# Cross attention of a decoder layer: keeping each batch's scores in SBUF and taking their maximum there, instead of scoring twice

## The chip, the cores and the metric

The kernel runs on 1 core of one Trainium2 chip. The metric is the device time of one execution in microseconds (us), the median over runs. A profiled execution gives the trace from which all rows below come.

## What is computed

The whole decoder layer is self attention (an LSTM makes Gaussian weights), cross attention, and a mixture of four experts chosen per token. The change touches the cross attention alone:

```python
# x: (32, 56, 128), ctx_1024: (32, 1500, 128), 16 heads of 64
q = (Q @ WQ).reshape(N, ql, HEADS, DK)
k = (K @ WK).reshape(N, kl, HEADS, DK)
v = (V @ WV).reshape(N, kl, HEADS, DV)
compat = jnp.einsum('nqhk,nlhk->nhql', q, k) / math.sqrt(DK)
weights = jax.nn.softmax(compat, axis=3)
attn = jnp.einsum('nhqk,nkhv->nqhv', weights, v).reshape(N, ql, HEADS * DV)
return attn @ WO + bO
```

Q is the normalized x, K and V are both the context. The kernel folds WQ with WK and WV with WO, so per batch the queries are a 128 x 896 matrix (16 heads x 56 queries = 896 columns) which is multiplied with the context itself.

## The kernel before

There are 32 batches, worked in 16 pairs (112 tokens); batch b = 2i + k belongs to pair i. The context of a batch, 1500 rows, is cut into 12 chunks of 125 rows (CH = 12, CR = 125), and the 896 columns into two halves of 448. One call of `period(i, k)` on each engine is one batch; it runs over 12 slots, one for each chunk. The first and the last pair are written out, the others are a loop. Each engine has its own instruction stream, and all order between engines is by semaphores (`need(engine, name, value)` waits).

For one batch the kernel before does this:

- **The maximum, from a scoring pass of its own, one batch ahead.** TensorE (`side("max")`, L598) multiplies the queries of batch b+1 with the context in 21 pieces (7 blocks of 128 columns x 3 parts of 500 rows), with the queries on the partitions, so that VectorE (`read_max`, L1252) can reduce each piece along the free dimension. VectorE then makes a diagonal of the 896 maxima (`max_diag`, L1259), TensorE spreads it over all partitions (L603), and ScalarE stores it negated (`negate_max`, L969).
- **The scores.** ScalarE copies the negated maxima into the PSUM banks of a chunk (`seed`, L976), TensorE adds the scores on top (`scores`, L717: three products of the fp32r high and low parts for each half), and ScalarE takes the exponential from PSUM into one of four SBUF buffers (`probs`, L1033).
- **The weighing.** TensorE multiplies the exponentials with the context (`weigh`, L729), one chunk behind the scores. GpSimd adds the exponentials up for the denominators (L447, L452), 11 additions for each batch.
- **Work beside it**, placed by two strings of letters, one for each batch of a pair, `PLACES`: twelve words are the twelve slots, and four letters in a word are the places after TensorE's four half products of the slot. `m` is a max piece, `t` a piece of turning the next context (L590; ScalarE L898 makes its high part, VectorE L1139 its low part), `q` the next queries (L629), `s` the denominators (L609), `p` the projection (L617; VectorE L1290 adds the heads), `d` the spread. All of these share PSUM banks 6 and 7 in turn: a piece waits until the piece before it in its bank was read (`side_banks`).

ScalarE and VectorE also each take half of the weighed sum out of PSUM once for each batch (`take_u`, L996 and L1267), and split the next queries (`query_hi`, L963; `query_lo`, L1244).

## Time and profile before

| | |
|---|---|
| median of 3 runs | 1717.54 us (1717.15 to 1722.96) |
| the profiled execution: time, span of the core | 1721.62 us, 1719.5 us |
| TensorE busy over the span | 96% |
| ScalarE, VectorE, GpSimd busy | 53%, 49%, 46% |
| TensorE's granted clock, mean | 0.975 |

The cross attention takes the time from about 185 us to about 1612 us. A matmul's record covers its latency too, so two matmuls that follow each other overlap in the trace; what one costs TensorE is read from the start of one to the start of the next, or from the pieces of the chain.

### The profile page before, as it was taken

How to read it: one execution, taken by the hardware profiler on the slowest of the kernel's cores; microseconds unless marked ns; L12 is line 12 of the kernel's file. 1: busy time of each engine (PE TensorE's matmuls, PEld its weight loads, DVE VectorE, ACT ScalarE, POOL GpSimd, SP SyncE). 2: the span in 40 equal slices, each digit the busy share in tenths (PEclk: the TensorE clock that was granted, in tenths of full speed). 3: DMA queues.
4: the chain of work that ended last, by engine and by line, in shares of the span. 5: the costliest groups of instructions: out<-in, count | busy, mean ns of one | idle time of the engine just before them, and what ended most of it. 6: DMA issues, size and time to landing. Idle time of an engine off the chain costs nothing.

```text
span 1719.5 us, 25064 instructions
## 1 busy us (share of the span) xinstructions
PE 1647.4 (96%) x7783; PEld 1181.7 (69%) x7783; DVE 843.5 (49%) x1772; ACT 918.7 (53%) x1311; POOL 792.1 (46%) x414
## 2 busy tenths in 40 slices
PE   6876999999999999999999999999999999998997
PEld 3344677777777777777777777767677777776664
DVE  3349445454545444454545445454454545454345
ACT  3233565656565656555555556565656565655211
POOL 2003454545454555545455555454545454545410
PEclk9996899999999999999999999999999999999788
DMA  4000000000000000001010101000000000000000
GB/s 150 25 17 2 1 36 37 36 36 36 36 36 36 36 36 36 36 29 43 18 45 15 44 20 40 31 36 36 36 36 36 36 36 36 36 18 1 1 1 22
DMA packets 15052, 54.84 MB, mean 32 GB/s; under 512 B 919, under 2 KB 6122, under 8 KB 15022
## 3 DMA queue, kind: packets, MB, share of 16 engines
q1 hardware_dynamic: 15022, 54.46, 8.4%
q8 instruction: 17, 0.28, 0.1%
q14 instruction: 13, 0.11, 0.0%
HBM read 53.54 MB, written 0.92 MB: 32 GB/s over the span
## 4 chain that ended last, share of the span: by engine, by line
PE 87%; DVE 8%; ACT 2%; issue 1%; POOL 1%; DMA 0%; DVEq 0%; POOLq 0%; ACTq 0%
PE ps L729 32%; PE ps L717 26%; PE ps L598 9%; PE ps L617 3%; PE ps L629 3%; PE ps L779 3%; PE ps L609 3%; PE ps L590 2%; DVE max_diag L1259 2%; PE ps L524 1%; DVE max_parts L1252 1%; PE ps L603 1%; DVE xnorm L1099 1%; ACT arena L877 1%; ACT arena L880 1%
## 5 line engine op out<-in xcount | busy, mean ns | idle before, releaser
L452 POOL TENSOR_TENSOR arena<-arena,probs 125x896 f32<-125x896 f32 x320 | 677.6, 2118 | 546.8 <-ACT probs L1033 456.6
L729 PE MATMUL ps<-probs,ctx_nat 125*128 125x448 f32 x1536 | 685.7, 544 | 0.0
L1252 DVE TENSOR_REDUCE max_parts<-ps 128x1 f32<-128x500 f32 x672 | 451.6, 676 | 354.7 <-PE ps L598 347.2
L1033 ACT ACTIVATE probs<-ps 125x896 f32<-125x896 f32 x384 | 351.6, 916 | 474.3 <-PE ps L717 430.9
L598 PE MATMUL ps<-ctxT_hi,q_hi 128*128 128x500 f32 x672 | 365.1, 544 | 2.2 <-DVE max_parts L1252 1.3
L976 ACT ACTIVATE ps<-arena 125x896 f32<-125x896 f32 x384 | 354.1, 922 | 7.9
L729 PEld LDWEIGHTS ps<-probs,ctx_nat 125*128 125x128 f32 x1536 | 277.6, 191 | 95.8 <-issue 79.7
L717 PE MATMUL ps<-q_hi,ctxT_hi 128*125 128x448 f32 x768 | 331.2, 431 | 1.8 <-ACT ps L976 1.8
L717 PE MATMUL ps<-q_lo,ctxT_hi 128*125 128x448 f32 x768 | 282.8, 368 | 0.0
L717 PE MATMUL ps<-q_hi,ctxT_lo 128*125 128x448 f32 x768 | 281.7, 367 | 0.0
L717 PEld LDWEIGHTS ps<-q_hi,ctxT_hi 128*125 128x125 f32 x768 | 144.5, 188 | 70.0 <-issue 62.1
L598 PEld LDWEIGHTS ps<-ctxT_hi,q_hi 128*128 128x128 f32 x672 | 127.4, 190 | 82.2 <-DVE max_parts L1252 29.7
L717 PEld LDWEIGHTS ps<-q_lo,ctxT_hi 128*125 128x125 f32 x768 | 144.2, 188 | 42.5 <-issue 22.1
L717 PEld LDWEIGHTS ps<-q_hi,ctxT_lo 128*125 128x125 f32 x768 | 143.2, 186 | 14.2
L447 POOL TENSOR_TENSOR arena<-probs 125x896 f32<-125x896 f32 x32 | 68.4, 2139 | 149.0 <-ACT probs L1033 149.0
L1139 DVE TENSOR_TENSOR ctxT_lo<-ps,ctxT_hi 128x500 fp32r<-128x500 f32 x96 | 64.4, 670 | 131.0 <-ACT ctxT_hi L898 131.0
L1244 DVE TENSOR_TENSOR q_lo<-arena,q_hi 128x896 fp32r<-128x896 f32 x32 | 38.8, 1212 | 92.8 <-ACT q_hi L963 92.8
L898 ACT ACTIVATE ctxT_hi<-ps 128x500 fp32r<-128x500 f32 x96 | 56.3, 587 | 45.9 <-PE ps L590 45.9
L617 PEld LDWEIGHTS ps<-vo_w,arena 128*112 128x112 f32 x512 | 64.0, 176 | 23.8 <-issue 23.8
L1290 DVE SCALAR_TENSOR_TENSOR resid<-ps,sum_recip,resid 112x128 f32 (+1 forms) x128 | 44.3, 346 | 63.6 <-PE ps L617 63.6
L629 PEld LDWEIGHTS ps<-xT,qk_w 128*128 128x128 f32 x512 | 67.1, 196 | 11.0 <-issue 9.1
L629 PE MATMUL ps<-xT,qk_w 128*128 (+1 forms) x512 | 69.3, 281 | 0.6 <-ACT xT L859 0.6
(186 smaller groups left out, 1259.6 us busy)
## 6 DMA issues: line engine op xcount, KB each, us to landing
ctx_raw<-in_ctx_dram SPq DMA_DIRECT2D x32, 750.0 KB
ctx_nat<-in_ctx_dram SPq DMA_DIRECT2D x32, 750.0 KB
w_sb<-in_L_ffn_W_dram SPq DMA_DIRECT2D x1, 1024.0 KB
resid<-in_x_dram SPq DMA_DIRECT2D x1, 896.0 KB, 6.7
out_dram<-ctx_raw SPq DMA_DIRECT2D x4, 224.0 KB, 2.5
ctx_raw<-in_L_xattn_WQ_dram SPq DMA_DIRECT2D x1, 512.0 KB
w_sb<-in_L_xattn_WK_dram SPq DMA_DIRECT2D x1, 512.0 KB
w_sb<-in_L_xattn_WV_dram SPq DMA_DIRECT2D x1, 512.0 KB
```

The lines of the kernel that those rows point to most:

```text
L447: g.tensor_tensor(first_sum if k == 0 else summed, chunk[0], chunk[1], ALU.add).then_inc(s["prob_added"], 1)
L452: g.tensor_tensor(summed, first_sum if j == 2 and k == 0 else summed, chunk[j % NP], ALU.add).then_inc(s["prob_added"], 1)
L598: mm(ps[:, bank, 0:MC], q_hi[nk][:, block_ * 128:(block_ + 1) * 128], ctxT_hi[nk][:, part * MC:(part + 1) * MC], start=True, stop=True).th ...
L617: m = mm(ps[0:TOK, bank, n * D:(n + 1) * D], u_sum[:, h].rearrange("p b q -> p (b q)"), vo_w[:, h, :], start=True, stop=True)
L629: m = mm(ps[:, bank, n * TOK:(n + 1) * TOK], qk_w[:, 4 * which + n, :], xT[:, bass.ds(i + 1, 1), :].rearrange("p k t -> p (k t)"), start=T ...
L717: m = mm(score_ps[j % 2][:, half, :], cx[k][:, rows], q[k][:, cols], start=False, stop=True, skip_group_check=True)
L729: m = mm(usum_ps[:, half, :], ctx_nat[k][:, j, :], probs[j % NP][:, half, :], start=(j == 0), stop=(j == CH - 1))
L898: a(ctxT_hi[k][:, which * MC:(which + 1) * MC], ps[:, bank, 0:MC], ACT.Copy).then_inc(s["ctxT_hi_done"], 1)
L976: a(score_ps[j % 2], neg_max[k][0:CR], ACT.Copy).then_inc(s["seeded"], 1)
L1033: a(probs[j % NP][:], score_ps[j % 2], ACT.Exp, scale=SCALE).then_inc(s["prob_done"], 1)
L1139: v.tensor_tensor(ctxT_lo[k][:, part], ps[:, bank, 0:MC], ctxT_hi[k][:, part].bitcast(F32), ALU.subtract).then_inc(s["ctxT_lo_done"], 1)
L1252: v.tensor_reduce(max_parts[:, which:which + 1], ps[:, bank, 0:MC], AX.X, ALU.max).then_inc(s["max_read"], 1)
```

## The change

The scoring pass for the maximum goes away. Each batch's scores are made once, copied to a ring of 12 SBUF buffers, and everything after works in that ring:

- **TensorE.** The twelve `scores` of batch b+1 run during the weighing of batch b. At the start of a period `turn_max` transposes the running maxima (8 transposes) into banks 6 and 7, `spread_max` (8 small matmuls against an identity) writes the found maxima over all 125 partitions into the same two banks, where they stay until the last subtraction has read them. After a slot's `weigh` comes `scores` of the chunk after it.
- **ScalarE.** `keep_scores` copies the scores of a chunk from PSUM to the ring in place of `seed`; `exponential` works in place in the ring.
- **VectorE.** `run_maximum` takes the maximum of `run_max` and a ring buffer, 11 for each batch (the last one reads PSUM); `find_max` reduces the turned maxima; `subtract_max` subtracts the maxima, which lie in PSUM, from each ring buffer, 12 chunks.
- **Order within a period.** ScalarE does `exponential` of chunks 0 and 1, then for each slot j `keep_scores(b + 1, j)` and the exponentials in `EXPS_AT[j]`. VectorE does the first four subtractions, then for each slot j from 1 `run_maximum(b + 1, j)` and the subtractions in `SUBS_AT[j]`.
- **Work beside it.** `PLACES` has no `m` and no `d` any more; the first piece is in slot 6. Queries are made two pairs ahead. The first batch's scores stand before the first period, and the last period has no scores.

```diff
-        PLACES = ("m..m mssm ssmm mmpm .mpm mmpm mmpm mqmm mqqt ..dd qt.. t...",
-                  "m..m mm.m mm.m mm.m m.m. m.m. m.mt m.m. m.mt ..dd .... .t..")
+        PLACES = (".... .... .... .... .... .... .t.t .t.p .p.p .p.. .... ....",
+                  ".... .... .... .... .... .... .t.t .t.q .q.q .qss ss.. ....")
+        EARLY = 4
+        SUBS_AT = {1: (4, 5), 2: (6,), 3: (7, 8), 4: (9,), 5: (10, 11)}
+        EXPS_AT = {0: (2, 3), **SUBS_AT}
...
         def side_banks(i, k):
...
+            before = {SIDE + n: ("subbed", STEPS * (2 * i + k + 1)) for n in range(2)}
...
             def scores(b, k, j, half):
...
-                    need(pe, "seeded", CH * b + j + 1)
+                    need(pe, "copied", CH * b + j - 1)
+                    if j == 1:
+                        need(pe, "maxed", (CH - 1) * b)
...
+            def keep_scores(b, j):
+
+                need(act, "scored", CH * b + j + 1)
+                if j == CH - 1:
+                    need(act, "maxed", (CH - 1) * (b + 1))
+                need(act, "weighted", CH * (b - 1) + j + 1)
+                need(act, "prob_added", (CH - 1) * (b - 1) + max(j, 1))
+                a(ring[j], score_ps[j % 2], ACT.Copy).then_inc(s["copied"], 1)
+
+            def exponential(b, j):
+
+                for part in ((slice(0, 1), slice(1, 2)) if j == 0 else (slice(0, 2),)):
+                    need(act, "subbed", step_count(b, j, part.stop - 1))
+                    a(ring[j][:, part], ring[j][:, part], ACT.Exp, scale=SCALE).then_inc(s["prob_done"], 1)
...
+                exponential(b, 0)
+                exponential(b, 1)
                 for j in range(CH):
...
+                    if j:
+                        side_copies(i, k, j - 1)
+                    if not last:
+                        keep_scores(b + 1, j)
+                    for n in EXPS_AT.get(j, ()):
+                        exponential(b, n)
...
+                for half in range(2):
+                    turn_max(i, k, half)
+                if not last:
+                    for half in range(2):
+                        scores(b + 1, 1 - k, 0, half)
+                for half in range(2):
+                    spread_max(b, half)
+                if not last:
+                    for half in range(2):
+                        scores(b + 1, 1 - k, 1, half)
                 for j in range(CH):
...
                     for half in range(2):
...
+                        weigh(i, b, k, j, half)
                         beside(j, half)
                     for half in range(2):
...
+                        if 1 <= j < CH - 1 and not last:
+                            scores(b + 1, 1 - k, j + 1, half)
                         beside(j, 2 + half)
...
+            def run_maximum(b, j):
+
+                if j < CH - 1:
+                    need(dve, "copied", CH * b + j + 1)
+                else:
+                    need(dve, "scored", CH * b + j + 1)
...
+                v.tensor_tensor(run_max, ring[0] if j == 1 else run_max, ring[j] if j < CH - 1 else score_ps[j % 2], ALU.max).then_inc(s["maxed"], 1)
...
+                for half in range(2):
+                    find_max(b, half)
+                if not first:
+                    take_u(i, k)
+                for j in range(EARLY):
+                    subtract_max(b, j)
+                for j in range(1, CH):
+                    if not (last_pair and k == 1):
+                        run_maximum(b + 1, j)
+                    for n in SUBS_AT.get(j, ()):
+                        subtract_max(b, n)
+                    late_turns(i, k, j - 1)
...
+                    side_reads(i, k, j, range(4))
```

How the instructions stand shows it. In each row the brackets name the semaphores waited for; ring buffers carry the names `arena`, `wo_raw` or `ring` after the memory they lie in. ScalarE before, in batch 1 (written out): a seed, L976, and an exponential, L1033, in turn.

```order
L976 ACTIVATE ps<-arena 125x2x448 [waits s_neg_done,s_prob_done]
L1033 ACTIVATE probs<-ps 125x896 [waits s_prob_added,s_weighted,s_scored]
L969 ACTIVATE arena<-ps 128x448 [waits s_spread_ps] x2
L976 ACTIVATE ps<-arena 125x2x448 [waits s_neg_done,s_prob_done]
L1033 ACTIVATE probs<-ps 125x896 [waits s_prob_added,s_weighted,s_scored]
```

ScalarE after, batch 1 from its start to slot 5: L989 is `keep_scores` of batch 2 (chunks 0, 1, 2, ...), L995 is `exponential` of batch 1.

```order
L1014 ACTIVATE arena<-ps 128x8x56 [waits s_weighted]
L995 ACTIVATE arena<-arena 125x448 [waits s_subbed] x2
L995 ACTIVATE arena<-arena 125x896 [waits s_subbed]
L989 ACTIVATE arena<-ps 125x896 [waits s_prob_added,s_weighted,s_scored]
L995 ACTIVATE arena<-arena 125x896 [waits s_subbed] x2
L989 ACTIVATE arena<-ps 125x896 [waits s_prob_added,s_weighted,s_scored]
L995 ACTIVATE arena<-arena 125x896 [waits s_subbed]
L995 ACTIVATE wo_raw<-wo_raw 125x896 [waits s_subbed]
L989 ACTIVATE arena<-ps 125x896 [waits s_prob_added,s_weighted,s_scored]
L995 ACTIVATE ring<-ring 125x896 [waits s_subbed]
L989 ACTIVATE arena<-ps 125x896 [waits s_prob_added,s_weighted,s_scored]
L995 ACTIVATE ring<-ring 125x896 [waits s_subbed] x2
```

What moved: the copies of the next batch now stand between the exponentials of this one, and each exponential waits for VectorE. VectorE before, in batch 1:

```order
L1267 COPY arena<-ps 128x8x56 [waits s_weighted]
L1252 TENSOR_REDUCE max_parts<-ps 128x1 [waits s_max_ps] x16
L1139 TENSOR_TENSOR ctxT_lo<-ps,ctxT_hi 128x500 [waits s_ctxT_hi_done]
L1252 TENSOR_REDUCE max_parts<-ps 128x1 [waits s_max_ps] x3
L1256 TENSOR_REDUCE max_all<-max_parts 128x7 [waits s_diag_done,s_max_read]
L1259 TENSOR_TENSOR max_diag<-ident,max_all 128x896 [waits s_spread_ps,s_max_found]
```

VectorE after, batch 1 from the third full subtraction: L1268 is `run_maximum` of batch 2 (chunks 1 to 5), L1282 is `subtract_max` of batch 1.

```order
L1282 TENSOR_TENSOR arena<-arena,ps 125x896 [waits s_spread_ps,s_copied] x3
L1268 TENSOR_TENSOR arena<-arena 125x896 [waits s_run_turned,s_copied]
L1282 TENSOR_TENSOR arena<-arena,ps 125x896 [waits s_spread_ps,s_copied]
L1282 TENSOR_TENSOR wo_raw<-wo_raw,ps 125x896 [waits s_spread_ps,s_copied]
L1268 TENSOR_TENSOR arena<-arena 125x896 [waits s_maxed,s_copied]
L1282 TENSOR_TENSOR ring<-ring,ps 125x896 [waits s_spread_ps,s_copied]
L1268 TENSOR_TENSOR arena<-arena 125x896 [waits s_maxed,s_copied]
L1282 TENSOR_TENSOR ring<-ring,ps 125x896 [waits s_spread_ps,s_copied] x2
L1268 TENSOR_TENSOR arena<-arena 125x896 [waits s_maxed,s_copied]
L1282 TENSOR_TENSOR ring<-ring,ps 125x896 [waits s_spread_ps,s_copied]
```

What moved: the 21 reductions from PSUM are gone; a maximum that waits for ScalarE's copy stands ahead of the subtractions for which ScalarE's exponentials wait. TensorE before, in slot 8 of batch 1: a turning piece (L590) waits for the reading of a max piece.

```order
L729 MATMUL ps<-probs,ctx_nat 128x448
L590 MATMUL ps<-ident,ctx_raw 128x125 [waits s_max_read]
L590 MATMUL ps<-ident,ctx_raw 128x125 x3
L717 MATMUL ps<-q_hi,ctxT_hi 125x448 [waits s_seeded]
L717 MATMUL ps<-q_lo,ctxT_hi 125x448
```

TensorE after, slots 6 and 7 of batch 1: L738 is `weigh`, L588 the turning piece, L704 `scores` of batch 2.

```order
L738 MATMUL ps<-ring,ctx_nat 128x448
L588 MATMUL ps<-ident,ctx_raw 128x125 [waits s_ctx_in1,s_subbed]
L588 MATMUL ps<-ident,ctx_raw 128x125 x3
L704 MATMUL ps<-q_hi,ctxT_hi 125x448 [waits s_copied]
...
L738 MATMUL ps<-ring,ctx_nat 128x448
L588 MATMUL ps<-ident,ctx_raw 128x125 [waits s_ctxT_lo_done]
L588 MATMUL ps<-ident,ctx_raw 128x125 x3
```

What moved: the first turning piece now waits for the last subtraction of the batch, with the scores of chunk 7 behind it, and the third waits for VectorE to have read the first.

## Rows read from the trace of the kernel before

**Rows 1.** The page: span, then busy time of each engine.
```profile
span 1719.5 us, 25064 instructions
PE 1647.4 (96%) x7783; PEld 1181.7 (69%) x7783; DVE 843.5 (49%) x1772; ACT 918.7 (53%) x1311; POOL 792.1 (46%) x414
```

**Rows 2.** Busy times in one pair of batches: stretch, length, engines, granted clock.
```profile
708.55:798.16 89.61, 89.35 (x409) 65.69 (x408) 44.14 (x77) 52.95 (x67) 46.57 (x23) 1.00 0.09 34
```

**Rows 3.** Chain that ended last, same pair: shares by line; pieces (start, us).
```profile
by line: PE ps L729 39.1%; PE ps L717 31.5%; PE ps L598 10.9%; PE ps L629 4.1%; PE ps L617 3.9%; PE ps L609 3.1%; PE ps L590 2.5%; DVE max_diag L1259 2.5%; PE ps L603 1.2%; DVE max_parts L1252 0.8%; issue 0.3%; DVE max_all L1256 0.2%; DVEq 
...
727.22 1.23 PE ps L717 x6
741.34 1.01 PE ps L629 x8
...
755.16 1.51 PE ps L729 x4
```

**Rows 4.** The same view of 715 to 722 us.
```profile
717.92 0.23 PE ps L598
718.15 0.61 PE ps L717 x3
718.75 0.69 PE ps L609 x8
```

**Rows 5.** Groups by line, 400 to 1600 us: busy us, mean ns; idle.
```profile
L452 POOL TENSOR_TENSOR arena<-arena,probs 125x896 f32<-125x896 f32 x268 | 567.1, 2116 | 458.5 <-ACT probs L1033 380.3 <-PE ps L609 76.8
L1252 DVE TENSOR_REDUCE max_parts<-ps 128x1 f32<-128x500 f32 x546 | 367.1, 676 | 290.3 <-PE ps L598 289.3
L976 ACT ACTIVATE ps<-arena 125x896 f32<-125x896 f32 x322 | 297.0, 922 | 6.5
L1033 ACT ACTIVATE probs<-ps 125x896 f32<-125x896 f32 x323 | 295.7, 916 | 399.7 <-PE ps L717 359.6 <-POOL arena L452 35.0 <-POOL arena L447 5.1
L1139 DVE TENSOR_TENSOR ctxT_lo<-ps,ctxT_hi 128x500 fp32r<-128x500 f32 x76 | 51.0, 671 | 104.7 <-ACT ctxT_hi L898 104.7
L963 ACT ACTIVATE q_hi<-arena 128x896 fp32r<-128x896 f32 x25 | 23.7, 949 | 0.0
L1267 DVE COPY arena<-ps 128x448 f32<-128x448 f32 x27 | 16.6, 614 | 9.4 <-PE ps L729 9.4
```

**Rows 6.** Timeline around 657 us: start us, us, engine, instruction.
```profile
656.60 1.09 DVE L1259 TENSOR_TENSOR max_diag<-ident,max_all 128x896 fp32r<-128x896 f32 x1
657.35 2.29 POOL L452 TENSOR_TENSOR arena<-arena,probs 125x896 f32<-125x896 f32 x1 [2.35 <-ACT probs L1033]
```

**Rows 7.** Timeline around 880 us.
```profile
878.95 2.10 POOL L452 TENSOR_TENSOR arena<-arena,probs 125x896 f32<-125x896 f32 x1 [1.33 <-ACT probs L1033]
879.80 2.21 DVE L1259 TENSOR_TENSOR max_diag<-ident,max_all 128x896 fp32r<-128x896 f32 x1
```

**Rows 8.** Timeline around 887 us, for the step from one engine to another.
```profile
885.03 0.90 ACT L1033 ACTIVATE probs<-ps 125x896 f32<-125x896 f32 x1
886.08 2.10 POOL L452 TENSOR_TENSOR arena<-arena,probs 125x896 f32<-125x896 f32 x1 [1.63 <-ACT probs L1033]
886.82 0.94 ACT L963 ACTIVATE q_hi<-arena 128x896 fp32r<-128x896 f32 x1
...
887.78 1.35 DVE L1244 TENSOR_TENSOR q_lo<-arena,q_hi 128x896 fp32r<-128x896 f32 x1 [5.18 <-ACT q_hi L963]
```

**Rows 9.** Busy times around a stall late in the cross attention; columns as in 2.
```profile
1560.00:1568.00 8.00, 8.00 (x30) 5.24 (x28) 3.25 (x11) 5.74 (x7) 4.93 (x4) 1.00 0.00 0
1568.00:1576.00 8.00, 3.75 (x10) 2.18 (x9) 6.46 (x17) 2.27 (x3) 3.77 (x3) 0.69 0.01 3
1576.00:1584.00 8.00, 8.00 (x31) 5.76 (x29) 1.57 (x1) 4.01 (x5) 4.62 (x3) 0.88 0.00 0
```

More of the change, by code:

```diff
@@ L581, in spread_mask, with turn, sums @@
                 mm(ps[:, mask_bank(e), 0:GT], pick_e[:, e, :], onehotT[n], start=True, stop=True).then_inc(s["mask_ps"], 1)
+            def turn(i, k, which, bank):
+                if which == 0:
+                    need(pe, f"ctx_in{k}", 16 * (i + 2))
+                for c in range(TG):
+                    m = tr(ps[:, bank, c * CR:(c + 1) * CR], ctx_in[k][:, which * TG + c, :], ident[0:CR, 0:CR])
+                m.then_inc(s["ctxT_ps"], 1)
+            def sums(pair, which, bank):
+                if which == 0:
+                    need(pe, "prob_added", (CH - 1) * 2 * (pair + 1))
+                for n in range(4):
+                    m = mm(ps[0:TOK, bank, n:n + 1], prob_sum[:, 4 * which + n].rearrange("p b q -> p (b q)"), ones[0:CR, 0:1], start=True, stop=True)
+                m.then_inc(s["sums_ps"], 1)
@@ new lines, in project, with query @@
+            def project(pair, which, bank):
+                if which == 0:
+                    need(pe, "u_act", 2 * (pair + 1))
+                    need(pe, "u_dve", 2 * (pair + 1))
+                for n in range(4):
+                    h = 4 * which + n
+                    m = mm(ps[0:TOK, bank, n * D:(n + 1) * D], u_sum[:, h].rearrange("p b q -> p (b q)"), vo_w[:, h, :], start=True, stop=True)
+                m.then_inc(s["projected"], 1)
+            def query(pair, which, bank):
+                for n in range(4):
+                    m = mm(ps[:, bank, n * TOK:(n + 1) * TOK], qk_w[:, 4 * which + n, :],
+                           xT[:, bass.ds(pair, 1), :].rearrange("p k t -> p (k t)"), start=True, stop=True)
+                m.then_inc(s["q_ps"], 1)
@@ L619, in side @@
+                    turn(i, k, which, bank)
+                elif what == "sums":
+                    sums(i, which, bank)
+                elif what == "project":
+                    project(i - 1, which, bank)
+                elif what == "query":
+                    query(i + 2, which, bank)
                 elif what == "tokens":
@@ L626, in side @@
                     spread_mask(0, which)
-                elif what == "query":
-                    for n in range(4):
-                        m = mm(ps[:, bank, n * TOK:(n + 1) * TOK], qk_w[:, 4 * which + n, :],
-                               xT[:, bass.ds(i + 1, 1), :].rearrange("p k t -> p (k t)"), start=True, stop=True)
-                    m.then_inc(s["q_ps"], 1)
             def beside_first(u):
@@ new lines, in find_max, with subtract_max @@
+            def find_max(b, half):
+                need(dve, "run_turned", 2 * b + half + 1)
+                need(dve, "spread_ps", 2 * (b - 1) + half + 1)
+                v.tensor_reduce(max_all[:, 4 * half:4 * half + 4], ps[0:QB, SIDE + half, 0:4 * CR].rearrange("p (n l) -> p n l", n=4),
+                                AX.X, ALU.max).then_inc(s["max_found"], 1)
+            def subtract_max(b, j):
+                need(dve, "copied", CH * b + j + 1)
+                for part in ((slice(0, 1), slice(1, 2)) if j == 0 else (slice(0, 2),)):
+                    need(dve, "spread_ps", 2 * b + part.stop)
+                    v.tensor_tensor(ring[j][:, part], ring[j][:, part], ps[0:CR, SIDE + part.start:SIDE + part.stop, 0:HALF],
+                                    ALU.subtract).then_inc(s["subbed"], 1)
@@ L1375, in side_reads @@
                 for what, which, bank in slot_work(i, k, j, places):
-                    if what == "max":
-                        read_max(i, k, which, bank)
-                    elif what == "sums":
-                        invert_sums(i - 1, which, bank)
+                    if what == "sums":
+                        invert_sums(i, which, bank)
                     elif what == "project":
```

340 lines of the change are left out of this document (128 added, 212 removed).

## The prediction

> **What bounds the kernel now.** I read the page first: TensorE is busy for 96% of the span and the others for about half [rows 1]. A busy TensorE can hide waits, so next comes one pair of batches by itself: 89.6 us, 44.8 for a batch, at the full granted clock, with ScalarE busy 53, GpSimd 47 and VectorE 44 us of it [rows 2]. The chain of that stretch says what the time is spent on: all but some 4% is matmul after matmul [rows 3]. The shares are costs without latency: six score products (one chunk) 1.23 us, four weighing passes (one chunk) 1.51 [rows 3], one max piece 0.23, four denominators 0.69 [rows 4]. For one batch: scores 12 x 1.23 = 14.8; weighing 12 x 1.51 = 18.1; max pieces 21 x 0.23 = 4.8; half of each pair's turning (2.5% of 89.6), denominators, projection and queries, 6.1; spread and the wait for `max_diag`, about 1. That is 44.8. TensorE is the bound, and nothing else comes near.
>
> **The change by sums.** TensorE loses the max pieces and the spread (-4.8, -0.5) and gains 8 transposes and 8 small matmuls. A turning transpose costs 0.09 (2.5% of 89.6 us over 24) [rows 3]; the small ones are not in the trace, between nothing and the same, together 0.8 to 1.6, and I take 1.3. TensorE's own work becomes 40.8 us. ScalarE trades each seed (0.92) for a copy of the same size. GpSimd keeps 11 additions of 2.12 [rows 5]. VectorE loses 21 x 0.68 and gains 11 maxima and 12 subtractions of 896 elements. From SBUF such an operation is 1.09 [rows 6]; from PSUM, 500 elements take 0.671 and 448 take 0.614 [rows 5], which carried on to 896 is also 1.1. With its other work VectorE has about 33 us. If sums decided, TensorE would still be the bound and the kernel 4 us faster for each batch. They do not, because of the order.
>
> **The change by its order.** Let time 0 be the end of batch b-1's last weighing. No engine can pass it: the maximum of b needs all its scores, and every exponential of b needs the maximum. I follow the three written orders from there. A copy or an exponential is 0.92, a maximum or a subtraction 1.09.
>
> *Turn-over, 12.6 us.* Chunk 10's copy goes into a buffer that the weighing frees just before, so copy 10, maximum 10 and maximum 11 (3.1) run against TensorE's scores 11 and weighing 11 (2.7): with the steps, a wait of 0.8. Then: first four transposes with their latency 0.65; two `find_max` reductions, as L1252, 1.36; `take_u` 0.61; subtraction 0 in halves 1.22; subtraction 1 1.09; exponential 1 0.92. The copy of the next chunk 0 overwrites buffer 0, which GpSimd's first addition still reads: 2.12 and 0.15 for the step to GpSimd (885.93 to 886.08) [rows 8]. Then copy 0, exponentials 2 and 3, copy 1: 3.67. Sum 12.4, and 0.2 for steps of 0.02 to 0.15 between engines [rows 8]. The scores of chunks 0 and 1 (2.5) hide in it.
>
> *Ping-pong, 24.0 us.* From slot 1 to 5 ScalarE and VectorE work in turn and hardly ever together: copy j frees maximum j, ahead of the subtractions; these free the exponentials, and they stand ahead of copy j+1. Slots 1, 3 and 5 cost maximum, two subtractions, exponential, copy: 5.11. Slots 2 and 4, with one subtraction, 4.02. That is 23.4, and 0.6 for ten steps. TensorE needs only 2.74 for a slot, but its scores j+1 wait for copy j-1, so it goes at 4.7. Subtraction 11 ends at 34.7. Only now may the first turning piece use bank 6, with scores 7 behind it: weighing 7 begins at 36.9.
>
> *Tail.* TensorE is the bound again: 5 weighings 7.55, 4 scores 4.9, one turning piece 0.4; projections of the first batch of a pair 3.5, or queries 4.0 and denominators 2.8 of the second. Twice a piece needs the bank of a turning piece that VectorE reads only behind its next maximum: after weighing 7, copy 7, maximum 7 and the low part (0.92 + 1.09 + 0.67 and steps) make 3.1, and the same once more in slot 8. The tail is 22.6 or 25.9.
>
> Batches end at 59.5 and 62.8, mean **61.1 us** where it was 44.8.
>
> *A lock.* `run_maximum` reads two SBUF operands while GpSimd adds. The nearest thing is `max_diag`: 1.09 alone, where a GpSimd addition that starts behind it takes 2.29 for 2.10 [rows 6], but 2.21 when the addition has begun, ending 1.0 after that ends [rows 7]. So a maximum can wait for the rest of an addition: nothing to 2.1 each. Where two exponentials precede it, the addition that the first one frees is just ending (0.1 to 0.3); after a single one it has about 1.2 left. Slots 1 to 5: 0.3, 0.1, 1.2, 0.1, 1.2, so 2.9; bounds 0 and 10.5. The Trainium skill, "SBUF — State Buffer", section "SBUF: two separate sides", says that VectorE with two SBUF inputs and GpSimd hold a shared port pair alternately, each for a whole instruction. By that rule the batch is 64.0, without it 61.1; both rows agree with it.
>
> *The clock.* Where TensorE is busy for 3.75 of 8 us, the granted clock falls to 0.69, and is 0.88 in the next 8 us: about 6.8 us at 1.2 instead of 2.4 GHz [rows 9]. Here TensorE sits idle for some 4.7 us in slot 6 and 3 us twice later. One such fall in a batch costs at most 3.4 us, none costs nothing, two 6.8; as part of the low time falls on waits, I take 1.5.
>
> **Sum.** 61.1 + 2.9 + 1.5 = 65.5 a batch, +20.7 for 31 of them, +642. The last period has no scores: 12 x 1.51 and its turn-over, about 23 us, where the old one has 12 x 2.74 = 33: -10. At the start, 12 scored chunks take the place of 21 exposed reductions of 0.68: 14.8 against 14.2, +1. The profiled execution took 1721.6 (span 1719.5), 4 over the median: 1721.6 + 633 - 4 = **2350 us**.
>
> **Rivals.**
> - *The sums decide* (the other side). If the twelve buffers let ScalarE copy so far ahead that the ping-pong hides, a batch is 40.8 and the kernel 1717.5 - 31 x 4 + a few, about 1600. For it: every engine's sum is under 41. Against: copy j+1 stands behind the exponentials of slot j. It decides only if slots 1 to 5 take under 2.8 us each; the smallest has 4.0 us of work in sequence. 4%.
> - *The ping-pong alone.* The bank waits (6.2) and the lock (2.9) turn out hidden, and the clock stays full: 54.9 a batch, +10.1 x 31 - 9, about 2020; halfway cases up to 2200. Against: the waits are in the orders of the program. 7%.
> - *The clock stays low.* At 1.2 GHz TensorE's 40.8 us become 82 and it is the bound: +37 x 31, up to 2870. For it: with 41 us of work in 61, TensorE waits far more than anywhere in the loop before, and one long stall cost the clock [rows 9]. Against: at 1.2 GHz it would be busy all the time, and in such a stretch the clock came back to full within 8 us [rows 9]. A mixture above 2480: 9%. The Trainium skill, "TensorE: Matmul & The Clock Gate", section "What's actually happening", says that the throttled clock is the default and activity releases it; the fall and the return in rows 9 agree.
> - *Nothing changes* (the two effects cancel): 1%.
>
> **Chances and range.** The forecast has 79%: slower, 2200 to 2480. Its low end leaves out lock and clock (-91 and -46) and a little more for a wait that is shorter; its high end has a second fall of the clock in each batch or 4 us more of lock waits. That is also the range for 8 in 10. A difference under 0.5% (9 us) can't be told from none here. Faster 4%, same 1%, slower 95%.
>
> **What would show it.** In the new profile: a pair takes 120 to 135 us; VectorE's idle time before `run_maximum` ends mostly with ScalarE's copy, and ScalarE's before the exponentials with VectorE's subtraction, 2 us each, five times a batch; `run_maximum` has a mean above 1.09 us and subtractions of 1.1; TensorE waits over 4 us for the subtraction ahead of the turning piece of slot 6; a granted clock below 1. I am wrong if ScalarE's copies run ahead of VectorE (a pair near 82 us), if maxima from SBUF take their 1.09 throughout, or if the clock's mean is under 0.8.

## The result and the profile after

| | before | after |
|---|---|---|
| median of 4 runs each | 1717.43 us | 2399.09 us (2394.02 to 2409.38) |
| ratio after : before, 95% interval | | 1.3966 (1.3912 to 1.402) |
| the profiled execution: time, span | 1721.62, 1719.5 us | 2409.38, 2407.7 us |

Slower by 40%; forecast were 2350 us and a range of 2200 to 2480. First the page of the changed kernel: span, busy times, the granted clock of TensorE in 40 slices, the chain's shares by engine, then three groups (count, busy us, mean ns, idle us before them and what ended it).

```profile
span 2407.7 us, 24704 instructions
PE 1805.5 (75%) x7555; PEld 1245.1 (52%) x7555; DVE 1299.6 (54%) x1868; ACT 893.1 (37%) x1279; POOL 869.8 (36%) x414
PEclk9978888898889898888989888998889888889778
issue 36%; PE 29%; DVE 17%; ACT 12%; POOL 3%; DVEq 1%; ACTq 1%; DMA 0%; POOLq 0%
L1268 DVE TENSOR_TENSOR arena<-arena,ring 125x896 f32<-125x896 f32 x160 | 184.2, 1151 | 415.5 <-ACT ring L989 415.4
L1268 DVE TENSOR_TENSOR arena<-arena 125x896 f32<-125x896 f32 x128 | 198.3, 1549 | 328.5 <-ACT arena L989 328.2
L995 ACT ACTIVATE ring<-ring 125x896 f32<-125x896 f32 x192 | 182.4, 950 | 363.1 <-DVE ring L1282 359.9
```

TensorE fell from 96% to 75% of a longer span [rows 1], and no other engine is above 54%: nothing is full, so engines wait for each other. The groups name the pair. `run_maximum` (L1268) waits 415 and 328 us for ScalarE's copies (L989), and the exponentials (L995) wait 363 us for VectorE's subtractions (L1282). One pair of batches, with the columns of [rows 2]:

```profile
1257.90:1391.00 133.10, 99.11 (x396) 68.47 (x394) 72.68 (x84) 51.33 (x65) 51.86 (x22) 0.88 0.06 23
```

133.1 us for 89.6 [rows 2], at a granted clock of 0.88 instead of 1.00. ScalarE's busy time is about what it was, VectorE's rose from 44 to 73 us. Two slots of one batch, from the timeline (start us, us, engine, instruction, idle time before it and what ended it):

```profile
1409.50 0.95 ACT L995 ACTIVATE ring<-ring 125x896 f32<-125x896 f32 x1 [2.42 <-DVE ring L1282]
1410.36 0.90 ACT L989 ACTIVATE arena<-ps 125x896 f32<-125x896 f32 x1
1410.61 2.10 POOL L453 TENSOR_TENSOR arena<-arena,ring 125x896 f32<-125x896 f32 x1 [0.19 <-ACT ring L995]
...
1411.38 2.28 DVE L1268 TENSOR_TENSOR arena<-arena 125x896 f32<-125x896 f32 x1 [1.91 <-ACT arena L989]
...
1413.59 2.07 DVE L1282 TENSOR_TENSOR ring<-ring,ps 125x896 f32<-125x896 f32 x2
1414.69 1.95 ACT L995 ACTIVATE ring<-ring 125x896 f32<-125x896 f32 x2 [3.44 <-DVE ring L1282]
1415.80 4.99 POOL L453 TENSOR_TENSOR arena<-arena,ring 125x896 f32<-125x896 f32 x2 [3.08 <-ACT ring L995]
1416.55 0.90 ACT L989 ACTIVATE arena<-ps 125x896 f32<-125x896 f32 x1
1417.50 0.74 PE L704 MATMUL ps<-q_hi,ctxT_hi 128*125 128x448 f32 x1 [3.20 <-ACT arena L989]
1417.57 1.27 DVE L1268 TENSOR_TENSOR arena<-arena 125x896 f32<-125x896 f32 x1 [1.91 <-ACT arena L989]
```

This is the ping-pong: VectorE sits idle 1.91 us until the copy ends (1411.26), takes the maximum and two subtractions, while ScalarE sits idle 3.44; ScalarE does two exponentials and the next copy, while VectorE sits idle 1.91. The maximum that starts at 1411.38 takes 2.28 us and ends 0.95 after the GpSimd addition that had begun before it (1410.61 + 2.10 = 1412.71), as `max_diag` did in [rows 7]. The later part of the same batch:

```profile
1426.13 0.64 PE L588 MATMUL ps<-ident,ctx_raw 125*128 125x125 f32 x4 [3.04 <-DVE ring L1282]
...
1429.11 2.97 DVE L1255 TENSOR_TENSOR q_lo<-arena,q_hi 128x896 fp32r<-128x896 f32 x1
...
1431.64 0.92 ACT L989 ACTIVATE ring<-ps 125x896 f32<-125x896 f32 x1 [1.20 <-PE ps L738]
1432.67 1.09 DVE L1268 TENSOR_TENSOR arena<-arena,ring 125x896 f32<-125x896 f32 x1 [0.59 <-ACT ring L989]
1433.68 1.25 DVE L1150 TENSOR_TENSOR ctxT_lo<-ps,ctxT_hi 128x500 fp32r<-128x500 f32 x2
1434.41 1.10 PE L588 MATMUL ps<-ident,ctx_raw 125*128 125x125 f32 x4 [2.89 <-DVE ctxT_lo L1150]
```

A turning piece waits 2.89 us for the low part (L1150), which stands behind the maximum, which waits for the copy, which waits for the weighing. TensorE's granted clock around it, by stretches of 8 us with the columns of [rows 2]:

```profile
1418.00:1426.00 8.00, 5.09 (x10) 2.66 (x8) 6.08 (x5) 2.71 (x3) 4.87 (x2) 0.67 0.00 0
1426.00:1434.00 8.00, 5.39 (x18) 3.83 (x18) 5.51 (x4) 4.58 (x6) 4.92 (x2) 0.76 0.00 0
1434.00:1442.00 8.00, 7.05 (x22) 5.40 (x22) 2.06 (x6) 1.01 (x2) 0.00 (x0) 0.60 0.00 0
1442.00:1450.00 8.00, 5.65 (x26) 4.92 (x27) 3.79 (x10) 0.49 (x1) 0.00 (x0) 0.79 0.00 0
```

The clock is low in every one of these stretches, also where TensorE is the bound (7.05 of 8 us busy at 0.60). The forecast's one fall of the clock in some batches is here a mixture of 1.2 and 2.4 GHz over the second half of the batch. Last, what TensorE waited for in the loop, 400 to 1600 us (us in total, times, longest); 18 batches end in it:

```profile
PE ps L704 <- ACT arena L989: 127.3, 62, 3.2
PE ps L588 <- DVE ring L1282: 70.8, 18, 5.6
PE ps L588 <- DVE ctxT_lo L1150: 52.5, 18, 2.9
PE ps L609 <- DVE ctxT_lo L1150: 26.5, 9, 2.9
PE ps L604 <- DVE ctxT_lo L1150: 26.0, 9, 2.9
```

By batch: 7.1 us for copies, 3.9 for the last subtraction, and two bank waits (a turning, query or projection piece that waits until VectorE has read the piece before it in its bank) of 2.9.

### The profile page after: what moved, and what is told of

Read it like the earlier page. It is cut to its first block, busy times and chain, and to the rows that moved or that the text cites. A ratio compares the mean times of both kernels' runs of the same rounds, so it can differ in the third digit from the quotient of the medians.

```text
span 2407.7 us, 24704 instructions
## 1 busy us (share of the span) xinstructions
PE 1805.5 (75%) x7555; PEld 1245.1 (52%) x7555; DVE 1299.6 (54%) x1868; ACT 893.1 (37%) x1279; POOL 869.8 (36%) x414
## 4 chain that ended last, share of the span: by engine, by line
issue 36%; PE 29%; DVE 17%; ACT 12%; POOL 3%; DVEq 1%; ACTq 1%; DMA 0%; POOLq 0%
PE ps L704 8%; DVE ring L1282 8%; PE ps L738 7%; ACT arena L989 5%; POOL arena L453 3%; PE ps L609 3%; ACT arena L995 3%; DVE arena L1282 2%; PE ps L588 2%; PE ps L797 2%; PE ps L595 2%; DVE wo_raw L1282 1%; ACT ring L989 1%; ACT wo_raw L989 1%; DVE arena L1268 1%
## 5 line engine op out<-in xcount | busy, mean ns | idle before, releaser
L453 POOL TENSOR_TENSOR arena<-arena 125x896 f32<-125x896 f32 x128 | 289.9, 2265 | 1085.2 <-ACT arena L995 1081.2
L704 PE MATMUL ps<-q_hi,ctxT_hi 128*125 128x448 f32 x768 | 376.2, 490 | 226.3 <-ACT arena L989 221.3
L453 POOL TENSOR_TENSOR arena<-arena,ring 125x896 f32<-125x896 f32 x192 | 445.5, 2320 | 204.6 <-ACT ring L995 197.0
L1268 DVE TENSOR_TENSOR arena<-arena,ring 125x896 f32<-125x896 f32 x160 | 184.2, 1151 | 415.5 <-ACT ring L989 415.4
L738 PE MATMUL ps<-ring,ctx_nat 125*128 125x448 f32 x768 | 376.8, 616 | 0.0
L1268 DVE TENSOR_TENSOR arena<-arena 125x896 f32<-125x896 f32 x128 | 198.3, 1549 | 328.5 <-ACT arena L989 328.2
L989 ACT ACTIVATE ring<-ps 125x896 f32<-125x896 f32 x192 | 175.7, 915 | 456.1 <-PE ps L738 408.7
L704 PEld LDWEIGHTS ps<-q_hi,ctxT_hi 128*125 128x125 f32 x768 | 167.8, 218 | 331.6 <-ACT arena L989 312.8
L704 PE MATMUL ps<-q_hi,ctxT_lo 128*125 128x448 f32 x768 | 325.4, 424 | 0.0
L704 PE MATMUL ps<-q_lo,ctxT_hi 128*125 128x448 f32 x768 | 325.2, 423 | 0.0
L995 ACT ACTIVATE ring<-ring 125x896 f32<-125x896 f32 x192 | 182.4, 950 | 363.1 <-DVE ring L1282 359.9
L738 PE MATMUL ps<-arena,ctx_nat 125*128 125x448 f32 x640 | 285.1, 571 | 3.4 <-ACT arena L995 1.1
L588 PE MATMUL ps<-ident,ctx_raw 125*128 125x125 f32 x384 | 92.1, 387 | 202.1 <-DVE ring L1282 114.8
L738 PEld LDWEIGHTS ps<-ring,ctx_nat 125*128 125x128 f32 x768 | 164.7, 229 | 92.0 <-issue 87.9
L995 ACT ACTIVATE arena<-arena 125x896 f32<-125x896 f32 (+1 forms) x192 | 153.5, 824 | 158.1 <-DVE arena L1282 158.0
L1282 DVE TENSOR_TENSOR ring<-ring,ps 125x896 f32<-125x896 f32 x192 | 201.1, 1074 | 0.0
L588 PEld LDWEIGHTS ps<-ident,ctx_raw 125*128 125x128 f32 x384 | 65.6, 201 | 259.9 <-DVE ctxT_lo L1150 109.2
L704 PEld LDWEIGHTS ps<-q_hi,ctxT_lo 128*125 128x125 f32 x768 | 172.1, 224 | 19.5
L704 PEld LDWEIGHTS ps<-q_lo,ctxT_hi 128*125 128x125 f32 x768 | 171.2, 223 | 20.0 <-issue 8.7
L738 PEld LDWEIGHTS ps<-arena,ctx_nat 125*128 125x128 f32 x640 | 126.3, 203 | 100.1 <-issue 63.9
L989 ACT ACTIVATE arena<-ps 125x896 f32<-125x896 f32 x160 | 144.8, 905 | 76.0 <-POOL arena L453 69.5
L1282 DVE TENSOR_TENSOR arena<-arena,ps 125x896 f32<-125x896 f32 (+1 forms) x192 | 167.0, 924 | 9.5 <-PE ps L726 9.3
```

The costliest lines, as they stand in the source:

```text
L453: g.tensor_tensor(summed, chunk[0] if j == 1 else summed, chunk[j], ALU.add).then_inc(s["prob_added"], 1)
L588: m = tr(ps[:, bank, c * CR:(c + 1) * CR], ctx_in[k][:, which * TG + c, :], ident[0:CR, 0:CR])
L704: m = mm(score_ps[j % 2][:, half, :], cx[k][:, rows], q[k][:, cols], start=(n == 0), stop=(n == 2))
L738: m = mm(usum_ps[:, half, :], ctx_nat[k][:, j, :], ring[j][:, half, :], start=(j == 0), stop=(j == CH - 1))
L989: a(ring[j], score_ps[j % 2], ACT.Copy).then_inc(s["copied"], 1)
L995: a(ring[j][:, part], ring[j][:, part], ACT.Exp, scale=SCALE).then_inc(s["prob_done"], 1)
```

## The experiments

Ten kernels, each a change of the changed kernel (2399 us). Beside them on their chips the kernel before took 1721.5 us (first four), 1722.09 (next four, median of 13) and 1722.05 (last two). All are single runs, except the last two of the middle four; the four runs of the changed kernel span 15 us, so a difference of that size between single runs shows nothing. Where a batch's parts are named, they are those of the table behind the last experiment.

**The maximum behind the subtractions (order only).**

```diff
                 for j in range(1, CH):
-                    if not (last_pair and k == 1):
-                        run_maximum(b + 1, j)
                     for n in SUBS_AT.get(j, ()):
                         subtract_max(b, n)
+                    if not (last_pair and k == 1):
+                        run_maximum(b + 1, j)
                     late_turns(i, k, j - 1)
```

> Only the order on VectorE changes: in each slot of a period the subtractions stand ahead of run_maximum; instructions, sizes and counts are the same. Order theory: the exponentials of a slot then need not wait for the copy and the maximum, so slots 1 to 5 (26 us in the new profile) fall to about 15 to 17 us, a batch from 66.5 to 56 to 58 us, the kernel to 2060 to 2160 us. Rival, VectorE's amount of work or its lock with GpSimd is what costs: the same instructions take the same time, 2370 to 2430 us.

Measured: **2097.61 us**, 301 less. Nothing but the order of two calls changed. Its groups of maxima:

```profile
L1268 DVE TENSOR_TENSOR arena<-arena,ring 125x896 f32<-125x896 f32 x160 | 259.6, 1622 | 350.5 <-ACT ring L989 350.4
L1268 DVE TENSOR_TENSOR arena<-arena 125x896 f32<-125x896 f32 x128 | 202.2, 1579 | 87.5 <-ACT arena L989 85.5
```

The wait of the second group (chunks 1 to 4, in the slots of the ping-pong) fell from 328 to 88 us; the first group's (chunks 6 to 10) lies mostly in the tail and went from 415 to 351. The ping-pong went from 26.05 to 14.2 us a batch, and the tail took 2.4 of that back. The lock went on: the first group's mean rose from 1.15 to 1.62 us.

**Maxima from PSUM, at the same place.** They still wait for the copy, and TensorE's next scores now wait for them.

```diff
                     need(pe, "copied", CH * b + j - 1)
-                    if j == 1:
-                        need(pe, "maxed", (CH - 1) * b)
+                    if j == 0:
+                        need(pe, "maxed", (CH - 1) * b - 1)
+                    elif j != 2:
+                        need(pe, "maxed", (CH - 1) * b + max(j - 2, 0))
...
-                v.tensor_tensor(run_max, ring[0] if j == 1 else run_max, ring[j] if j < CH - 1 else score_ps[j % 2], ALU.max).then_inc(s["maxed"], 1)
+                v.tensor_tensor(run_max, ring[0] if j == 1 else run_max, score_ps[j % 2], ALU.max).then_inc(s["maxed"], 1)
```

> run_maximum waits for the copy as before but reads the chunk's scores from PSUM instead of the ring, so it has one SBUF operand; TensorE writes a score bank again only when it was also read by the maximum. Order theory: run_maximum has 1.1 us throughout, 3 us less in slots 1 to 5 and about 1 later, a batch 62 to 64 us, the kernel 2260 to 2330 us. Rival, the lock is the main cost: most of the 22 us that a batch lost come back, under 2000 us.

Measured: **2226.16 us**, 173 less and a little below the range, at a clock of 0.940 where the changed kernel had 0.871. The maxima took 1.09 us. The ping-pong got 3.05 us a batch shorter, 95 us in all, which is the lock; the rest of the gain lies mostly in the tail, at a higher clock (0.96 and 0.91 for 0.90 and 0.84) and with waits for low parts as long as before (6.1 us a batch for 5.8). Why the clock was higher here is not shown.

**Small additions.** Ten of a batch's eleven GpSimd additions add only 8 columns, so most of the denominators is left out; the first addition, for which ScalarE's copy waits, is whole.

```diff
-                    g.tensor_tensor(summed, chunk[0] if j == 1 else summed, chunk[j], ALU.add).then_inc(s["prob_added"], 1)
+                    (g.tensor_tensor(summed, chunk[0], chunk[j], ALU.add) if j == 1 else g.tensor_tensor(summed[:, 0:1, 0:8], summed[:, 0:1, 0:8], chunk[j][:, 0:1, 0:8], ALU.add)).then_inc(s["prob_added"], 1)
```

> Leaves out work: of GpSimd's 11 additions for each batch the first is whole, the other ten add 8 columns only, so the denominators are not the reference's. Every wait stays. Order theory: the lock's part goes, in the maxima and in query_lo (2.97 us in the new profile where it is 1.09 alone), together 4 to 6 us a batch: 2210 to 2290 us. Rival, the lock or GpSimd is the main cost: under 2000 us. Rival, neither matters because VectorE catches up: 2370 to 2430 us.

Measured: **2308.25 us**, 91 less: missed. The lock was gone (the two groups on its page):

```profile
L1268 DVE TENSOR_TENSOR arena<-arena,ring 125x896 f32<-125x896 f32 x160 | 174.8, 1093 | 509.7 <-ACT ring L989 509.5
L1268 DVE TENSOR_TENSOR arena<-arena 125x896 f32<-125x896 f32 x128 | 139.8, 1092 | 328.5 <-ACT arena L989 328.2
```

but its granted clock was 0.860, lower than the changed kernel's. By itself this run could not say whether the lock is worth only 91 us or the clock took some of it back; the ninth and tenth kernels were made for that.

**The low parts first.** `late_turns` ahead of the maximum and the subtractions of its slot.

```diff
                 for j in range(1, CH):
+                    late_turns(i, k, j - 1)
                     if not (last_pair and k == 1):
...
                         subtract_max(b, n)
-                    late_turns(i, k, j - 1)
```

> Only the order on VectorE changes: in each slot the low parts of the turned context stand ahead of run_maximum and the subtractions. Order theory of the tail: the third turning piece waits 1 us less and the second query or projection piece not at all (2.9 in the new profile), 3.5 to 4.5 us a batch, 2260 to 2300 us. Rival, the tail is TensorE's work at the low clock, and the waits only hide in it: 2370 to 2410 us.

Measured: **2181.32 us**, 218 less, more than expected. TensorE's waits for low parts, of the same stretch as above (20 batches here):

```profile
PE ps L588 <- DVE ctxT_lo L1150: 17.0, 17, 1.6
PE ps L604 <- DVE ctxT_lo L1150: 5.0, 10, 0.5
```

That is 1.1 us a batch for 5.8, so 4.7 x 31 = 146 us are the waits. The other 70 are not waits of this kind. The ping-pong is what it was (26.05), and the tail got 7.1 us a batch shorter while its clock rose (0.94 for 0.90 and 0.84), so a bank wait seems to cost its own length and, behind it, some matmuls at 1.2 GHz. That the wait is what lowers the clock is argued, not shown.

**TensorE kept busy in its waits.** 81 small matmuls a batch into an unused part of a bank. The expectations say 97, which is wrong: the numbers of `WARMERS` add up to 81, each of which is two passes in the trace (12577 instructions of TensorE for 7555, 162 more in each of 31 batches).

```diff
+        WARMERS = (0, 7, 0, 10, 6, 15, 15, 14, 14, 0, 0, 0)
...
                         weigh(i, b, k, j, half)
+                        if half == 1 and not last:
+                            for n in range(WARMERS[j]):
+                                mm(ps[:, 4, HALF:512], ident[:], ident[:, 0:512 - HALF], start=False, stop=False, skip_group_check=True)
                         beside(j, half)
```

> Adds work: where TensorE waited 1.2 to 3.2 us in slots 1 and 3 to 8 it makes 6 to 15 small matmuls (64 columns, into unused columns of PSUM bank 4), 97 in a batch. Nothing else changes. Clock as a cost of its own: the granted clock rises from 0.87 towards 1 and the tail of a batch (29.7 us where its work and waits at the full clock make 24.3) gets 4 to 6 us shorter: 2210 to 2290 us. Rival, the low clock only fills waits: 2390 to 2430 us, since the small matmuls take some time.

Measured: **2337.0 us**, 62 less, between the two theories, at a clock of 0.947. More work made the kernel faster, so the clock does cost time, and it costs it in the tail: the ping-pong stayed at 26.1 us. How much it costs in all, this run leaves open, since the small matmuls take time too.

**Subtractions, low parts, maximum: both orders together.**

```diff
                 for j in range(1, CH):
-                    if not (last_pair and k == 1):
-                        run_maximum(b + 1, j)
                     for n in SUBS_AT.get(j, ()):
                         subtract_max(b, n)
                     late_turns(i, k, j - 1)
+                    if not (last_pair and k == 1):
+                        run_maximum(b + 1, j)
```

> The two changes of order on VectorE together: in each slot subtractions, then low parts, then run_maximum; the same instructions. Apart they took 301 and 218 us off 2399. Order theory: both waits go, and with them much of the time at the low clock, 1850 to 1980 us; the lock remains. Rival, they overlap: not under 2040 us.

Measured: **1875.71 us**, 523 less, about the sum of the two orders (301 + 218). Of the 680 us that the change cost, three quarters go by moving one call behind two others.

**The maximum before the copy.** The written orders are those of the changed kernel. The maximum reads PSUM as soon as a chunk is scored, and the copy waits for it (run e7_max_before_copy). TensorE's waits are those of the second experiment.

```diff
                 need(act, "scored", CH * b + j + 1)
-                if j == CH - 1:
-                    need(act, "maxed", (CH - 1) * (b + 1))
+                if j:
+                    need(act, "maxed", (CH - 1) * b + j)
...
-                if j < CH - 1:
-                    need(dve, "copied", CH * b + j + 1)
-                else:
-                    need(dve, "scored", CH * b + j + 1)
+                need(dve, "scored", CH * b + j + 1)
                 if j == 1:
+                    need(dve, "copied", CH * b + 1)
...
-                v.tensor_tensor(run_max, ring[0] if j == 1 else run_max, ring[j] if j < CH - 1 else score_ps[j % 2], ALU.max).then_inc(s["maxed"], 1)
+                v.tensor_tensor(run_max, ring[0] if j == 1 else run_max, score_ps[j % 2], ALU.max).then_inc(s["maxed"], 1)
```

> The order on VectorE and ScalarE is that of the changed kernel. Only what run_maximum reads changes: the chunk's scores in PSUM as soon as they are made, with the copy to the ring behind it (for every chunk, as the changed kernel does it for the last). So VectorE no longer waits for ScalarE's copy, and the lock goes. Order theory: slots 1 to 5 are no ping-pong any more, TensorE (40.8 us of work for a batch) is the bound but for the turn-over: 44 to 47 us a batch, 1700 to 1800 us. Rival, the copy that now waits for the maximum is a ping-pong of its own: over 2000 us.

Measured: **1731.63 us** (median of 10 runs), ratio to before 1.0054 (1.0032 to 1.0075). One of the ten took 2916.48 us and is left out of the comparison, the others 1728.57 to 1735.80; its clock was 0.895, no trace of it exists, and its cause is open. VectorE in the slots of the ping-pong, from its timeline:

```profile
1236.35 1.08 DVE L1282 TENSOR_TENSOR arena<-arena,ps 125x896 f32<-125x896 f32 x1
1237.35 1.08 DVE L1282 TENSOR_TENSOR wo_raw<-wo_raw,ps 125x896 f32<-125x896 f32 x1
1238.35 1.08 DVE L1268 TENSOR_TENSOR arena<-arena,ps 125x896 f32<-125x896 f32 x1
1239.34 1.08 DVE L1282 TENSOR_TENSOR ring<-ring,ps 125x896 f32<-125x896 f32 x1
1240.34 1.08 DVE L1268 TENSOR_TENSOR arena<-arena,ps 125x896 f32<-125x896 f32 x1
```

No idle time at all: a maximum every 2.0 to 3.0 us, where it was 4.2 to 6.2. The order of VectorE's program is the same as in the slow kernel. Two things differ, the lock is gone and the maximum no longer waits for ScalarE's copy; the second experiment has the first of them alone, at 2226 us, so the wait for the copy is worth the other 494, with what the clock gave back in them.

**Both: the maximum before the copy, and behind the subtractions and low parts.** The edits of the last two together.

> As e7_max_before_copy, and in each slot on VectorE subtractions, low parts, then run_maximum. If the waits that are left in slots 6 to 8 go, a batch comes to 42.5 to 45 us and the kernel to 1650 to 1720 us, faster than the kernel before. If the turn-over (about 11 us, with 5 us of TensorE's work in it) stays the bound, 1720 to 1780 us.

Measured: **1687.39 us** (4 runs, 1683.72 to 1691.38), ratio to before **0.9801 (0.9758 to 0.9843)**: it beats both kernels, the kernel before by some 2%. Its page, and one pair (columns of [rows 2]):

```profile
span 1681.9 us, 25214 instructions
PE 1541.8 (92%) x7555; PEld 1084.7 (64%) x7555; DVE 1142.8 (68%) x1868; ACT 867.3 (52%) x1279; POOL 810.9 (48%) x414
```
```profile
1235.80:1323.60 87.80, 83.64 (x394) 59.96 (x393) 62.43 (x83) 49.64 (x65) 47.87 (x22) 1.00 0.09 35
```

The idea of the change, scores made once, is sound: 87.8 us a pair for 89.6. TensorE is busy for 83.6 of them, where the prediction's sum for a pair was 81.6.

**The two missed ones together: small additions and the small matmuls,** with the edits shown and the same part left out as in the third experiment.

> The changed kernel with both edits of the two kernels that fell between their theories: 10 of the 11 GpSimd additions of a batch add 8 columns only (so the output misses most of the denominators), and 97 small dummy matmuls a batch are added in TensorE's waits. Alone the first gave 2308 us at a granted clock of 0.860, the second 2337 us at 0.947. Theory (the lock's saving of the first was partly eaten by a lower clock): with the clock held up the two savings together are larger than their sum of 153 us: 2150 to 2220 us, clock above 0.93. Rival (the small additions save 91 us and no more, whatever the clock): 2240 to 2260 us.

Measured: **2165.95 us**, 233 less, where the two alone gave 91 and 62. Its page's busy times and clock:

```profile
PE 2085.8 (96%) x12577; PEld 1653.1 (76%) x12577; DVE 1131.4 (52%) x1868; ACT 890.0 (41%) x1279; POOL 179.0 (8%) x414
PEclk9979999999999999999999999999999999999989
```

Beside the small matmuls the small additions are worth 2337 - 2166 = 171 us. 95 of them are the lock in the ping-pong, 3.05 us a batch, the same as without the small matmuls. The rest is in the tail. Alone, the small additions made the tail of a pair's second batch longer, with the same number of matmuls and at a lower clock (one such tail of the changed kernel, then one of the third; columns of [rows 2]):

```profile
1357.87:1390.95 33.08, 27.13 (x128) 20.86 (x127) 11.74 (x14) 8.91 (x13) 3.27 (x2) 0.84 0.00 0
1437.88:1473.34 35.46, 29.57 (x128) 23.01 (x127) 9.67 (x15) 8.85 (x13) 0.00 (x0) 0.74 0.00 0
```

In the mean of both batches the tail got 0.7 us longer, which took back some 20 of the 95 us. Not all of the 171 is the lock, though: from the fifth kernel to this one the tail's clock rose too (0.93 and 0.98 to 1.00). And the small matmuls (L778) make 25% of the chain that ended last here, so they can cost time themselves; what this kernel shows of the clock's cost is a lower bound:

```profile
PE ps L778 25%; PE ps L739 23%; PE ps L705 20%; PE ps L610 3%; PE ps L605 3%; DVE arena L1286 2%; PE ps L801 2%; PE ps L596 2%; PE ps L589 2%; DVE arena L1272 2%; PE ps L719 2%; ACT arena L999 1%; PE ps L525 1%; ACT ring L993 1%; PE ps L727 1%
```

**Maxima from PSUM with the small matmuls.**

> The changed kernel with maxima that wait for the copy as before but read the scores from PSUM, and the 97 small dummy matmuls a batch. Alone the first gave 2226 us at a granted clock of 0.940. Theory (what the reading from PSUM gave beyond the small additions was the clock, so with the clock held up both come to about the same time): 2160 to 2230 us, within 40 us of the kernel with small additions and dummy matmuls; the dummy matmuls give it little, since its clock is high already. Rival (the dummy matmuls give the same 62 us whatever else is changed): 2164 us here while the kernel with small additions stays at 2246.

Measured: **2214.3 us**, 12 less than without them, which two single runs can't tell from nothing and which fits the theory (the clock was high already, 0.940), but 48 us from the ninth, a little outside the 40 expected. Turn-over and ping-pong are the same in both; each tail is 1.0 us longer here, 31 of the 48 us. What differs in it includes the `q_lo` operation (two SBUF inputs in both), which has a mean of 2.47 us here and 1.08 there, and TensorE's wait for the maxima, 0.7 us a batch; how the 1.0 us divides was not tried.

**The parts of a batch in the kernels whose maximum waits for the copy.** Means over the whole batches from 400 to 1600 us, in us, with the tail's granted clock in brackets. A batch is divided at the start of the first reduction of `find_max`, the end of copy 1 and the end of copy 6. The first part, most of the turn-over, is 10.8 in all of them.

| | ping-pong | tail, first batch of a pair | tail, second batch |
|---|---|---|---|
| the changed kernel | 26.05 | 27.7 (0.90) | 32.8 (0.84) |
| 1: maximum behind the subtractions | 14.2 | 31.7 (0.84) | 33.6 (0.87) |
| 2: maxima from PSUM | 23.0 | 26.3 (0.96) | 30.1 (0.91) |
| 3: small additions | 23.0 | 26.5 (0.92) | 35.5 (0.74) |
| 4: low parts first | 26.05 | 22.2 (0.94) | 24.1 (0.94) |
| 5: small matmuls | 26.1 | 27.3 (0.93) | 28.7 (0.98) |
| 6: both orders | 14.2 | 24.3 (0.93) | 25.8 (0.96) |
| 9: small additions, small matmuls | 23.0 | 24.8 (1.00) | 27.6 (1.00) |
| 10: maxima from PSUM, small matmuls | 23.0 | 25.8 (1.00) | 28.6 (1.00) |

The ping-pong goes by the order and the lock alone: it is the same at a clock of 0.84 as at 0.95 (changed and fifth kernel), and at 0.86 as at 1.00 (third and ninth). What the clock costs lies in the tail, and the changed kernel's own trace shows it: its first batches have two kinds of tail, with the same matmuls and the same waits for low parts, 4.1 us apart (columns of [rows 2]):

```profile
1427.79:1458.18 30.39, 23.82 (x94) 17.78 (x93) 16.11 (x28) 6.78 (x9) 3.27 (x2) 0.79 0.01 1
1294.73:1320.99 26.26, 19.70 (x94) 14.19 (x93) 16.10 (x28) 6.79 (x9) 3.26 (x2) 0.96 0.01 1
```

## Why the prediction held, point by point

**The sums do not decide, the order does: right.** The first rival named the ping-pong as what stood against it. With the lock gone and the clock held up (ninth experiment, its 81 added matmuls included) the kernel took 2166 us; the forecast's order terms alone, 61.1 a batch, give 1722 + 16.3 x 31 - 9 = 2218. The batches of that kernel were 58.6 and 61.5 us for 59.5 and 62.8.

**The parts of one batch.** The batch whose rows stand above runs from the end of one last weighing (1390.10) to the next (1456.71), 66.6 us; it is the first of a pair, forecast at 59.5 + 2.9 + 1.5 = 63.9.

| | forecast | measured |
|---|---|---|
| turn-over, to the end of copy 1 | 12.6 | 11.6 |
| ping-pong with lock, to the end of copy 6 | 24.0 + 2.9 | 26.1 |
| tail | 22.9 + 1.5 of clock | 28.9 |

This batch has one of the longer tails: four of the nine first batches in the loop are like it, five are 4.1 us shorter, and the second batches have the longest. Over the loop, divided as in the table above, a mean batch has 10.8 + 26.05 + 30.3. The forecast, divided so (the 0.8 and 0.65 ahead of `find_max` go to the tail before), has 11.15 + 26.9 + 27.5. So the first two parts came out 1.2 us under and the tail 2.8 over, 1.6 a batch or some 50 us in all: the number is closer than its terms, because the errors lay on both sides.

- *Turn-over and ping-pong.* Both a little shorter than forecast. Instructions that follow each other on VectorE or ScalarE start about 0.1 us before the recorded end of the one ahead (exponential 1409.50 + 0.95 = 1410.45, copy at 1410.36), which the sum counted in full, and the step of 0.12 (1411.26 to 1411.38) lies within the 0.02 to 0.15 assumed.
- *The lock.* The five maxima of the slots took 1.45, 1.25, 2.28, 1.27 and 2.26 us, so 0.36, 0.16, 1.19, 0.18 and 1.17 above 1.09: 3.1 for the forecast's 0.3, 0.1, 1.2, 0.1, 1.2. As a mean of the loop the ping-pong is 3.05 us longer than without the lock. That the addition is what they wait for is shown by the third experiment (1.09 throughout), that the reading from SBUF matters by the second. The Trainium skill, "SBUF — State Buffer", section "SBUF: two separate sides", says that VectorE with two SBUF inputs and GpSimd hold the pair alternately, each for a whole instruction; both experiments agree.
- *The bank waits.* Forecast 3.1 each, measured 2.9, two in each batch.
- *The clock: right in sign, mis-sized.* The term was 1.5 us a batch (one fall in some batches). The nearest thing to a measurement is the step from the third to the ninth experiment: 142 us, at least 4.6 a batch, within the bounds of 0 to 6.8. The mean tail is 4.3 above a forecast without clock, about the same. The term that was mis-sized is the number of falls: the estimate took one stall as one fall, in some batches; the rows show the low clock in all stretches from 1418 to 1450, where waits of 2 to 3 us come again and again. That these keep it low is argued, though filling them raised it to 0.988. The Trainium skill, "TensorE: Matmul & The Clock Gate", section "What's actually happening", says that the throttled clock is the default and activity releases it. A kernel made faster by added matmuls (62 us here, 142 with the small additions) agrees with it.
- *Lock and clock do not add.* The forecast has 2.9 + 1.5 = 4.4 a batch, 136 us; together they measured 233. Removed one at a time they gave 91 and 62; the prediction's ledger, like the expectations of the third and fifth experiments, treated them as independent terms. The lock's part in the ping-pong does add, 3.05 us with or without the small matmuls; the tail is where the two meet.

So 2399 came out 49 above the forecast: lock and clock 97 over, the order 52 under, and 4 because the forecast is against a median of 1717.5, and these steps against the 1722 of the kernel before beside them. These are single runs, and the 233 includes `q_lo`, which the forecast's lock leaves out.

**The signs.** A pair took 133 us (forecast 120 to 135). Idle before maxima and exponentials 1.9 to 3.4 us. The turning piece of slot 6 was to wait over 4 us: 3.04 in the batch shown, 3.9 as a mean, 5.6 at most, so this sign was just missed; the low clock lengthened the matmuls ahead of it and so ate some of the wait. The maxima's means were 1.15 and 1.55 us, above 1.09, the subtractions' 1.07, and the clock's 0.871 lies below 1 and above 0.8, as said. Not foreseen was `q_lo`, whose 2.97 us show the lock at a sixth place; in the batch shown it lay beside the weighing and the maximum behind it still waited 0.59 us for its copy.

## What to carry to other kernels

Compare busy sums last: where two in-order engines each do a producer's and a consumer's step in every slot, write both orders down in time and look for an instruction that waits for the other engine and stands ahead of what that engine waits for. Here moving it back took away 523 of 680 us, and having it read its input before the copy instead of after took away 667 with both written orders as they were (173 of them come with the lock's end). Waits on TensorE can cost more than their length, because its clock can fall too: here 4.7 us of waits a batch fewer gave 7.0. Size them together with what else makes it wait, not as separate terms.

## What the runs showed of the hardware beside that

- A VectorE operation with two SBUF inputs took 1.09 us alone, up to 2.28 behind one GpSimd addition, and 2.97 at `q_lo`. A GpSimd addition behind a maximum took 2.82 where it takes 2.10 alone (mean 2.68 for 192 of them with the maximum behind the subtractions), so the lock costs on both sides:

```profile
1407.22 1.25 DVE L1268 TENSOR_TENSOR arena<-arena 125x896 f32<-125x896 f32 x1 [1.93 <-ACT arena L989]
1407.60 2.82 POOL L453 TENSOR_TENSOR arena<-arena,wo_raw 125x896 f32<-125x896 f32 x1
```

- Subtractions, with one input from SBUF and one from PSUM, kept 1.07 to 1.08 us beside the same additions, and the maxima took 1.08 to 1.09 once they read the scores from PSUM.
- Taking away the lock lowered the mean clock (0.871 to 0.860) and gave 91 us; 81 matmuls a batch of no use raised it (to 0.947) and gave 62. A time saved beside TensorE can't be read off without its clock.
